# Weight preparation in shorter units over more rounds: a vision transformer on one core

## The chip, the core and the metric

The kernel runs on one core of one Trainium2 chip. The metric is the device time of one execution in microseconds (us). TensorE (PE) multiplies matrices into PSUM banks, VectorE (DVE), ScalarE (ACT) and GpSimd (POOL) work elementwise, SyncE (SP) issues the transfers; each engine runs its own instructions in order and waits on semaphores for the others.

## What is computed

64 images of 3x224x224 go through a small vision transformer: patches to 197 tokens of width 192, a first block (an attention with 64 queries and 133 keys, then an MLP whose weights are masked by mixed coefficients), and a second block (12-head attention, then a quantised MLP). Cut to what matters here:

```python
h = L0_tok(x)                                     # 64 x 197 x 192
h = h + L0_attn(layernorm(h))
h = h + L0_ffn(layernorm(h))                      # W0 = w_fc * C0, W1 = w_proj * C1
h = h + L1_attn(layernorm(h))                     # W_qkv, W_0
h = h + L1_ffn(layernorm(h))                      # clip(round(w / alpha)) for both weights
# C0 = sum over i, j of alpha_e[i] * alpha_r[j] * (row < r * e) * (col < e), C1 likewise
```

The weights are inputs, so their masks, sums, quantisation and splits are computed in the kernel as well. A value of 32 bits enters a product as a high part in 16 bits and a low part (value minus high part).

## The kernel before

`h` stays in SBUF for all images. Four stages follow one another: `embed_attend` (the fused stage: patch embedding and first attention), `mlp_0` (first MLP), `attention_1` and `mlp_1`. The first two handle two images in a round, 32 rounds each, and every engine has an order of jobs that it repeats each round, written out by hand (`PE_ORDER`, `ACT_ORDER`, `DVE_ORDER`, `POOL_ORDER`). A mark behind a job's name shifts it: `'` means that it handles the pair of one round later, `^` the pair of one round earlier. `rounds` writes these rounds out: those at the start and the end one by one, those between as a loop of two rounds a turn. Work that is not part of the rounds, the weight preparation, is hung behind a job as a unit: `{"a1": {6: mask_fp}}` runs `mask_fp` behind the job a1 of pair 6. The written-out part reaches to the last unit; the loop begins behind it.

In the fused stage ACT's h0 and h1 round the patches of image 0 and 1 to 16 bits (L357), POOL's l00 to l12 form their low parts in three operations an image (L314), PE's E0 and E1 multiply them (L442), VectorE's a0 and a1 add the position and write `h` (L596), b0 and b1 take statistics (L603) and r aggregates them (L612). Once in two rounds, for the odd pair, POOL waits behind l11 for r (L325, a_var) and computes the reciprocal root in fifteen small steps q1 to q15, with l12 behind q5; q15 ends with a_my. The attention jobs follow some rounds later: VectorE's m (maximum, L621, which waits for PE's scores s, L465), x, p, o, t, i, f, s. VectorE's order is `b1^ r^ i s f m x a0 p b0 o t a1`, so a unit behind a1 stands ahead of b1 and r.

The raw weights of that stage lie in the part of `h` that the rounds have not written yet, from image `RAW_FROM` on. SP loads two images a round and, behind given rounds, the raw masks and the quantisation inputs. ACT makes the high parts of the masked weights (`high_fc`, `high_fp`), VectorE the low parts (`low_fc`, `low_fp`).

In `mlp_0` VectorE's order is `n' w0 .. w5 x' f^`: x (L891, L892) takes the turned input from PSUM, the unit comes behind it, then f adds the result to `h` (L902), n normalises the next pair (L115, L117) and w forms low parts of the hidden values (L896). Units prepare the quantised weights of `mlp_1` (`scales` to `split_bias`; the last one releases SP's load of the raw qkv weights), then the low parts of the qkv weights (L874) and of the output weights (L867), whose high parts come from ACT's `high_qkv` and `high_wo` (L931), hung behind ACT's job u.

## Time and profile before

| | |
|---|---|
| median of 3 runs (lowest, highest) | 2665.69 us (2665.47, 2665.91) |
| the profiled execution, its span | 2663.56 us, 2661.8 us |
| PE busy | 2483.4 us (93%) |
| weight loads of PE (beside it) | 2115.2 us (79%) |
| DVE busy | 2208.2 us (83%) |
| ACT busy | 2087.4 us (78%) |
| POOL busy | 1088.0 us (41%) |
| mean granted TensorE clock | 0.975 |
| fused stage, first MLP | about 0 to 399 us, 399 to 800 us |

The profile is one execution. The span runs from its first instruction to its last; the execution's own time holds some 1.8 us around it. The granted clock is 1.00 at 2.4 GHz and 0.5 at 1.2 GHz; between them it is a mean over a stretch. Busy shares are means over four stages with different limits, so they don't say what a change in one of them is worth. "Idle before <- X" tells how long an engine had nothing to do before an instruction and what ended it.

### The profile page before, as it was taken

How to read it: one execution, taken by the hardware profiler on the slowest of the kernel's cores; microseconds unless marked ns; L12 is line 12 of the kernel's file. 1: busy time of each engine (PE TensorE's matmuls, PEld its weight loads, DVE VectorE, ACT ScalarE, POOL GpSimd, SP SyncE). 2: the span in 40 equal slices, each digit the busy share in tenths (PEclk: the TensorE clock that was granted, in tenths of full speed). 3: DMA queues.
4: the chain of work that ended last, by engine and by line, in shares of the span. 5: the costliest groups of instructions: out<-in, count | busy, mean ns of one | idle time of the engine just before them, and what ended most of it. 6: DMA issues, size and time to landing. Idle time of an engine off the chain costs nothing. (4 is left out here: it accounts for less than half of the span.)

```text
span 2661.8 us, 83340 instructions
## 1 busy us (share of the span) xinstructions
PE 2483.4 (93%) x27552; PEld 2115.2 (79%) x27552; DVE 2208.2 (83%) x5761; ACT 2087.4 (78%) x6199; POOL 1088.0 (41%) x1501
## 2 busy tenths in 40 slices
PE   5899968999997999999999999999999999997877
PEld 4788856877876888888888888888888888885665
DVE  6767668988766888888888888888888888886997
ACT  3777757777756888888888888888888888886998
POOL 6777723333322334333433433433333433441333
PEclk9999978999998999999999999999999999997999
DMA  5334400010002333333333333333333333330111
GB/s 176 104 109 117 120 23 9 0 45 0 0 0 64 76 78 72 68 82 68 68 82 68 69 81 69 72 77 73 72 73 77 72 70 80 70 69 10 44 42 50
DMA packets 181839, 173.22 MB, mean 65 GB/s; under 512 B 19206, under 2 KB 180432, under 8 KB 181520
## 3 DMA queue, kind: packets, MB, share of 16 engines
q1 hardware_dynamic: 181776, 172.44, 27.3%
q8 instruction: 32, 0.52, 0.1%
q14 instruction: 31, 0.25, 0.0%
HBM read 46.49 MB, written 9.68 MB: 21 GB/s over the span
## 5 line engine op out<-in xcount | busy, mean ns | idle before, releaser
L1347 POOL TENSOR_TENSOR b_pr<-b_pr,b_rinv 128x394 f32<-128x394 f32 (+1 forms) x768 | 626.2, 843 | 1006.6 <-DVE b_rinv L1305 1006.6
L1242 ACT ACTIVATE b_pr<-b_banks,b_nmx 128x197 f32<-128x197 f32 (+1 forms) x1536 | 625.9, 424 | 27.8 <-DVE b_nmx L1299 25.3
L1213 ACT ACTIVATE b_pt<-b_bank_t 128x394 f16<-128x394 f32 (+1 forms) x768 | 338.0, 494 | 202.6 <-PE b_bank_t L1178 202.4
L1299 DVE TENSOR_REDUCE b_nmx<-b_banks 128x2 f32<-128x394 f32 (+1 forms) x768 | 397.3, 558 | 65.2 <-PE b_banks L1168 57.1
L1270 DVE TENSOR_TENSOR b_pt<-b_bank_t,b_pt 128x394 f16<-128x394 f32 (+1 forms) x768 | 395.9, 556 | 18.2 <-ACT b_pt L1213 18.1
L1152 PE MATMUL b_banks<-b_xt,wqkv 128*128 128x197 f16 x3840 | 373.9, 249 | 4.4 <-DVE b_xt L1270 2.2
L1178 PE MATMUL b_bank_t<-ident,b_pr 128*128 128x128 f32 (+3 forms) x3072 | 341.9, 253 | 3.1 <-DVE b_pt L1270 3.0
L1152 PEld LDWEIGHTS b_banks<-b_xt,wqkv 128*128 128x128 f16 x3840 | 320.9, 98 | 25.6 <-issue 18.8
L1168 PE MATMUL b_banks<-b_kst,b_qst 128*128 128x197 f16 (+1 forms) x3072 | 326.8, 248 | 6.7 <-ACT b_pr L1242 4.6
L1178 PEld LDWEIGHTS b_bank_t<-ident,b_pr 128*128 128x128 f32 (+3 forms) x3072 | 282.1, 142 | 43.1 <-issue 35.3
L1242 ACT ACTIVATION_READ_ACCUMULATOR b_pr<-b_banks,b_nmx 128x1 f32 (+1 forms) x1536 | 315.6, 205 | 0.0
L1168 PEld LDWEIGHTS b_banks<-b_kst,b_qst 128*128 128x128 f16 (+1 forms) x3072 | 266.0, 105 | 19.4 <-issue 14.1
L1192 PE MATMUL b_bank_o<-b_pt,b_val 128*64 128x197 f16 (+1 forms) x4608 | 272.4, 253 | 0.1
L442 PE MATMUL tokens<-tok_w,parts 128*128 128x192 f16 (+1 forms) x2304 | 210.6, 253 | 56.4 <-POOL parts L314 56.4
L442 PEld LDWEIGHTS tokens<-tok_w,parts 128*128 128x128 f16 (+1 forms) x2304 | 196.8, 109 | 66.7 <-POOL parts L314 47.4
L923 POOL TENSOR_TENSOR h<-h,fp_bias 69x192 f32 (+3 forms) x128 | 133.4, 1071 | 278.0 <-DVE m_xn L117 278.0
L1289 DVE SCALAR_TENSOR_TENSOR b_qk<-b_banks,b_qk 128x394 f16<-128x394 f32 x384 | 209.6, 560 | 45.1 <-ACT b_qk L1227 31.6
L1192 PEld LDWEIGHTS b_bank_o<-b_pt,b_val 128*64 128x64 f16 (+1 forms) x4608 | 187.0, 110 | 75.0 <-issue 29.7
L1159 PE MATMUL b_banks<-wqkv,b_xt 128*128 128x384 f16 (+1 forms) x1280 | 242.5, 328 | 0.7 <-DVE b_qk L1289 0.4
L1227 ACT ACTIVATE b_qk<-b_banks 128x394 f16<-128x394 f32 x384 | 189.2, 507 | 33.2 <-PE b_banks L1152 28.4
L314 POOL TENSOR_TENSOR parts<-patches,parts 128x394 f16<-128x394 f32 x192 | 185.8, 998 | 49.4 <-ACT parts L357 49.4
L1202 PE MATMUL b_banks<-wo,b_ot 128*128 128x192 f16 (+1 forms) x2304 | 203.2, 248 | 1.3 <-DVE b_ot L1270 1.3
(227 smaller groups left out, 4429.3 us busy)
## 6 DMA issues: line engine op xcount, KB each, us to landing
b_qst<-b_qk SPq DMA_DIRECT2D x512, 147.8 KB, 2.6
b_kst<-b_qk SPq DMA_DIRECT2D x512, 73.9 KB, 2.3
patches<-in_x SPq DMA_DIRECT2D x64, 588.0 KB, 4.2
out<-z_res SPq DMA_DIRECT2D x32, 192.0 KB
out<-z_res SPq DMA_DIRECT2D x32, 103.5 KB
m_raw_weights<-in_wqkv SPq DMA_DIRECT2D x2, 1152.0 KB, 6.4
m_raw_weights<-in_w SPq DMA_DIRECT2D x2, 576.0 KB, 5.3
h<-in_fc SPq DMA_DIRECT2D x1, 768.0 KB, 5.8
```

The costliest lines, as they stand in the source:

```text
L442: last = t.matmul(tokens[m][0:ROWS[c], c * D:(c + 1) * D], parts[m][:, pa, k, COLS[c]], tok_w[:, pb, k, :], start=(k == 0 and n == 0), sto ...
L1152: last = t.matmul(out[:, g * SEQ:(g + 1) * SEQ], w[:, (2 * n + g) * P:(2 * n + g + 1) * P], x, start=(j == 0), stop=(j == 4))
L1159: last = t.matmul(out[0:ROWS[c], 0:VH], x[:, COLS[c]], w[:, col:col + VH], start=(j == 0), stop=(j == 4))
L1168: last = t.matmul(banks[0:ROWS[c], c, e * SEQ:(e + 1) * SEQ], qst[:, part, e, n, COLS[c]], kst[:, e, n, :], start=(part == 0), stop=(part ...
L1178: last = t.transpose(bank_t[0:ROWS[kc], kc, e * SEQ + c * P:e * SEQ + c * P + ROWS[c]], pr[n % 3][0:ROWS[c], c, e, COLS[kc]], S["ident"][0 ...
L1192: last = t.matmul(bank_o[e * DH:(e + 1) * DH, b, lo:lo + SEQ], val[odd][0:ROWS[kc], pa, kc, head * DH:(head + 1) * DH], pt[n % 2][0:ROWS[k ...
L1213: return nc.scalar.activation(dst, src, ACT.Copy)
L1242: last = nc.scalar.activation(pr[n % 3][0:ROWS[c], c, e, :], banks[0:ROWS[c], c, e * SEQ:(e + 1) * SEQ], ACT.Exp, bias=nmx[n % 2][0:ROWS[c ...
L1270: return v.tensor_tensor(dst, src, high, ALU.subtract)
L1289: v.scalar_tensor_tensor(out=qk[:, 1, :, n], in0=banks[:, k, 0:2 * SEQ].rearrange("p (g t) -> p g t", g=2), scalar=QK_SCALE, in1=qk[:, 0, ...
L1299: v.reduce_max(nmx[n % 2][0:ROWS[c], c, :], banks[0:ROWS[c], c, 0:2 * SEQ].rearrange("p (e t) -> p e t", e=2), AX.X, negate=True).then_inc ...
L1347: last = nc.gpsimd.tensor_tensor(p, p, inv, ALU.mult)
```

## The change

It moves the units and divides some of them.

- Fused stage, VectorE: units behind a0 in rounds 2 to 4 and behind a1 in rounds 1 to 11 become one unit a round behind a1, rounds 6 to 19. ACT's `high_fc` and `high_fp` go from rounds 7 and 9 to 14 and 16; SP's mask loads from behind round 1 to behind round 3, the quantisation loads from 3 to 5. The raw weights begin at image 38 instead of 14 and take the room of 24 images instead of 50.
- First MLP, VectorE: `scales`, both divisions, both quantisations and `split_bias` are divided, with the same instructions in the same order but for the two limits, which now come ahead of both roundings; 18 units where there were 11, behind x of pairs 1 to 18 instead of 1 to 11. The low parts of the qkv weights go from pairs 14 to 17 to 22 to 25, that of the output weights from 19 to 28.
- First MLP, ACT: the scaling of the keys in two units, behind u of pairs 21 and 22 instead of one behind 14; `high_qkv` from 15 to 18 to 23 to 26; `high_wo` from 20 to 28.
- What follows from `rounds`: VectorE's loop in the fused stage begins at round 20 instead of 12, ACT's at 17 instead of 10; in the first MLP, where they began at round 19, fewer than two turns are left and neither engine has a loop any more.

```diff
-    h, RAW_FROM, RAW_SIZE = S["h"], 14, 50 * 2 * D
+    h, RAW_FROM, RAW_SIZE = S["h"], 38, 24 * 2 * D
...
-                rounds(sp, ["d"], count, load, {"d": {1: load_masks, 3: load_quantised}}, first=3)
+                rounds(sp, ["d"], count, load, {"d": {3: load_masks, 5: load_quantised}}, first=3)
...
-                rounds(act, ACT_ORDER, count, job, {"h1": {7: high_fc, 9: high_fp}}, first=2)
+                rounds(act, ACT_ORDER, count, job, {"h1": {14: high_fc, 16: high_fp}}, first=2)
...
-                first_slot = {2: coefficient(1), 3: coefficient_sum(0), 4: hidden_columns}
-                second_slot = {1: coefficient(0), 2: coefficient(2), 3: coefficient_sum(1), 4: mask_fc, 5: mask_fc_bias, 6: mask_fp, 7: mask_fp_bias,
-                               8: low_fc(0), 9: low_fc(1), 10: low_fp, 11: means}
+                first_slot = {}
+                second_slot = {6: coefficient(0), 7: coefficient(1), 8: coefficient(2), 9: coefficient_sum(0), 10: coefficient_sum(1), 11: hidden_columns,
+                               12: mask_fc, 13: mask_fc_bias, 14: mask_fp, 15: mask_fp_bias, 16: low_fc(0), 17: low_fc(1), 18: low_fp, 19: means}
...
-                def divide_first():
-                    for k in range(2):
-                        then(v.tensor_tensor(r_w1[:, k], r_w1[:, k], a_w1[:], ALU.mult))
...
+                def divide_first(k):
+                    return lambda: then(v.tensor_tensor(r_w1[:, k], r_w1[:, k], a_w1[:], ALU.mult))
+
+                def divide_second(half):
+                    def make():
+                        for k in range(3 * half, 3 * half + 3):
+                            then(v.tensor_tensor(r_w2[:, k], r_w2[:, k], a_w2[:], ALU.mult))
+                    return make
...
-                units = {1: scales, 2: invert_rows(0), 3: invert_rows(1), 4: invert_rows(2), 5: invert_rows(3), 6: divide_first, 7: divide_second,
-                         8: quantise(0), 9: quantise(1), 10: sum_second, 11: split_bias, 19: low_wo}
-                units.update({14 + n: low_qkv(n) for n in range(4)})
+                units = {1: scales, 2: invert_scale, 3: invert_rows(0), 4: invert_rows(1), 5: invert_rows(2), 6: invert_rows(3), 7: divide_first(0),
+                         8: divide_first(1), 9: divide_second(0), 10: divide_second(1), 11: limit(0), 12: limit(1), 13: quantise(0), 14: quantise(1),
+                         15: sum_second, 16: divide_bias, 17: split_bias, 18: pick_bias, 28: low_wo}
+                units.update({22 + n: low_qkv(n) for n in range(4)})
...
-                        act.wait_ge(keys_scaled, 1)
+                        act.wait_ge(keys_scaled, k + 1)
...
-                rounds(act, ACT_ORDER, count, job, {"u": {14: scale_keys, 20: high_wo, **{15 + n: high_qkv(n) for n in range(4)}}}, first=2)
+                rounds(act, ACT_ORDER, count, job, {"u": {21: scale_keys(0), 22: scale_keys(1), 28: high_wo, **{23 + n: high_qkv(n) for n in range(4)}}}, first=2)
```

## Rows read from the trace of the kernel before

**Rows 1.** Windows by pair: length, busy PE PEld DVE ACT POOL (count), PEclk, DMA, GB/s.
```profile
34.34:59.86 25.52, 15.26 (x172) 14.27 (x172) 19.18 (x47) 11.88 (x19) 19.09 (x34) 0.93 0.35 97
59.86:82.92 23.06, 19.11 (x214) 17.25 (x215) 16.93 (x71) 13.19 (x26) 17.64 (x34) 0.85 0.37 106
82.92:106.42 23.50, 20.00 (x261) 17.86 (x259) 19.12 (x68) 17.89 (x33) 16.93 (x33) 1.00 0.37 104
128.80:152.75 23.95, 21.66 (x260) 19.41 (x258) 17.60 (x68) 16.43 (x32) 16.83 (x33) 0.93 0.36 101
152.75:174.32 21.57, 18.39 (x222) 16.37 (x221) 14.70 (x61) 14.01 (x27) 15.55 (x33) 0.92 0.34 96
174.32:194.76 20.44, 19.04 (x249) 16.90 (x247) 14.26 (x61) 15.88 (x31) 15.70 (x33) 1.00 0.41 117
```

**Rows 2.** Timeline of VectorE in a clean odd round: start, length, instruction, idle before.
```profile
208.59 0.30 DVE L621 TENSOR_REDUCE mx<-bank_s 128x1 f32<-128x133 f32 x1 [3.03 <-PE bank_s L465]
...
214.68 0.38 DVE L612 BATCH_NORM_AGGREGATE mv<-st 128x2 f32<-128x6 f32 x4
```

**Rows 3.** Timeline of GpSimd: a_var of the first pair, and a clean pair's first steps.
```profile
34.34 0.20 POOL L325 TENSOR_TENSOR a_var<-mv,a_eps 128x8 f32<-128x8 f32 x1 [1.72 <-DVE mv L612]
...
215.20 0.20 POOL L325 TENSOR_TENSOR a_var<-mv,a_eps 128x8 f32<-128x8 f32 x1 [0.43 <-DVE mv L612]
...
222.68 5.23 POOL L314 TENSOR_TENSOR parts<-patches,parts 128x394 f16<-128x394 f32 x6
```

**Rows 4.** Timeline of TensorE: E0 behind the clean pair's root steps.
```profile
225.38 3.14 PE L442 MATMUL tokens<-tok_w,parts 128*128 128x192 f16 x36 [1.01 <-POOL parts L314]
```

**Rows 5.** The tile parts over the fused stage: count, duration ns min/median/max, forms.
```profile
L314 POOL TENSOR_TENSOR parts<-patches,parts x192: 902/912/2812, 11.9 to 349.6; 128x394 f16<-128x394 f32 x192
L357 ACT ACTIVATE parts<-patches x64: 1173/1191/1192, 10.5 to 344.3; 128x1182 f16<-128x1182 f32 x64
```

**Rows 6.** Windows over eight units, VectorE alone: length, busy DVE (count), PEclk, DMA, GB/s.
```profile
29.89:33.03 3.14, 3.03 (x5) 1.00 0.76 239
34.62:36.66 2.04, 1.93 (x5) 1.00 0.00 0
43.46:47.53 4.07, 3.96 (x5) 1.00 0.27 55
50.04:54.23 4.19, 4.11 (x4) 1.00 0.45 138
55.32:58.56 3.24, 3.17 (x4) 1.00 0.57 181
61.47:64.89 3.42, 3.31 (x19) 0.54 0.00 0
70.82:72.56 1.74, 1.74 (x4) 1.00 0.59 143
80.04:81.66 1.62, 1.51 (x4) 1.00 0.60 136
```

**Rows 7.** Windows of the first MLP, from x' to x', columns as in the first.
```profile
426.51:775.02 348.51, 342.26 (x3205) 279.00 (x3203) 289.79 (x733) 258.33 (x529) 124.76 (x116) 1.00 0.02 9
438.92:473.85 34.93, 34.93 (x333) 28.72 (x332) 31.25 (x76) 26.04 (x55) 12.96 (x13) 1.00 0.01 1
520.42:559.59 39.17, 36.82 (x332) 29.95 (x331) 33.74 (x88) 26.04 (x55) 12.96 (x13) 0.96 0.16 60
571.23:633.68 62.45, 59.10 (x553) 47.57 (x551) 50.85 (x127) 47.61 (x95) 21.61 (x21) 1.00 0.03 10
633.68:646.43 12.75, 12.19 (x117) 9.82 (x115) 10.42 (x26) 9.72 (x20) 4.31 (x5) 1.00 0.00 1
646.43:763.45 117.02, 117.02 (x1103) 95.28 (x1101) 91.19 (x241) 86.81 (x181) 43.21 (x41) 1.00 0.00 0
```

**Rows 8.** Waits of VectorE in the first MLP: total us, times, longest us.
```profile
DVE wqkv L874 <- ACT wqkv L931: 7.5, 4, 1.9
DVE wo L867 <- ACT wo L931: 1.9, 1, 1.9
```

28 lines of the change are left out of this document (14 added, 14 removed).

## The prediction

> **What bounds the kernel now.** I read the profile in this order: the busy table and the granted clock for the whole span, then the stretches (busy time by window), then the timeline of the two stages that the change touches, then the waits of VectorE there. TensorE is busy 93% of the span, but not evenly, and the change touches only the first 800 us. About what a measurement of this kernel can tell from no change is 0.2%, here 5.3 us. The sum is made against the profiled execution (2663.56 us, span 2661.8); the median of the runs is 2.1 us above it, and I carry a difference in span over to the median unchanged.
>
> *Fused stage.* One round handles two images, and the norm statistics are handed to GpSimd once in two rounds, so I count in pairs, from one start of a_var (L325) to the next. A pair without units takes 20.44 us; the ones before it, which carry units or their aftermath, take 21.57 to 25.52 (six of them, five shown) [rows 1]. The clean pair shows which chain closes. TensorE's scores end and release VectorE's maximum at 208.59, after 3.03 us of idling; from there VectorE works without a pause through m, x, a0, p, b0, o, t, a1, b1 to the aggregate of r at 214.68 to 215.06 [rows 2]. GpSimd starts a_var at 215.20, works through the root steps until 222.68 and on into six parts operations [rows 3]; TensorE's next E0 starts when the third of them is done, at 225.38, and waited 1.01 us for it [rows 4]. From m to there it is 16.8 us; E0's 3.1 [rows 4] and the scores behind it close the loop at 20.4. That loop is the stage, and it has no slack where a1's unit of an **odd** round stands. A unit behind a1 of an **even** round stands between mv of r and the next m, where VectorE idles 3.03 us [rows 2]; it costs nothing up to that size, unless it slows GpSimd's parts operations, which it runs beside. These take 0.91 us at the median and up to 2.81 [rows 5].
>
> *First MLP.* VectorE is not the bound: in three rounds with a reciprocal unit each TensorE is busy all 34.93 us, 11.64 a round; ten loop rounds without units take 117.02, 11.70 each [rows 7].
>
> **The change, part by part.** *Taken out of rounds 1 to 4 (fused).* The units are measured as stretches in the first stage: coefficients 3.14, 2.04 and 4.07 us, the sums 4.19 and 3.24, hidden_columns 3.42, mask_fc 1.74 and mask_fc_bias 1.62 [rows 6]. Gone from these rounds, a_var of the first pair comes 1.7 us earlier (its whole idle time) [rows 3]. The next pair falls from 25.52 to about 20.0: the pipeline is still filling and VectorE's long chain is not there, so the lower end is 10.2 from a_var to E0 [rows 3, 4], E0 and E1 at 3.1, ACT's copy at 1.2 and two parts operations at 0.91 [rows 5], 19.5 in all; the clean 20.44 is the upper end, the one after from 23.06 to 20.44 [rows 1]. Together -9.8 us, bounds -8.5 to -10.5.
>
> *Put into rounds 6 to 12, one unit a round.* Here the pipeline is full. Even slots: coefficient(0) in 6 overflows its 3.03 us by 0.1 and slows a parts operation a little, 0.3; coefficient(2) in 8, 4.07 - 3.03 = 1.0; coefficient_sum(1) in 10, up to 4.19 beside GpSimd, 1.1; mask_fc in 12 fits, 0.3. Odd slots pay in full: coefficient(1) in 7, 2.0; coefficient_sum(0) in 9, 4.19 beside a busy GpSimd, but here GpSimd has run out of work and waits for VectorE, so 3.1 (3.24 for the same work as coefficient_sum(1), partly undisturbed [rows 6]); hidden_columns in 11, 3.4; mask_fc_bias in 13, 1.6 [rows 6] (before, in round 5, it was part of the 23.06). Sum 12.8. The longer odd units also open a TensorE gap behind which the granted clock falls to its lower level for a while, which shows as 0.92 or 0.93 in the pair: the pair of 21.57 has no unit at all, only that, and is 1.1 us over the clean one [rows 1]. Whether each of the three longest new ones brings one is not sure; three at 0.9 are 2.7. Eight more rounds of VectorE run unrolled instead of looped: -0.4 by the 0.055 a round of the MLP. Together +15.1, bounds +11 (sums at their undisturbed length, no lower clock) to +19.
>
> *Rounds 13 to 19.* Behind mask_fc_bias, mask_fp, mask_fp_bias, low_fc twice, low_fp and means follow one another in slots of the same parity as before in 6 to 11. So the four pairs that follow (82.92 to 174.32) are repeated eight rounds later and displace four clean ones: 0, give or take 1.5. ACT's high_fc and high_fp now come two rounds ahead of what reads them, and no wait was seen before. On SP's queue the seven mask loads move behind the patch load of round 3, and the four others behind that of 5: the transfers keep the DMA engines 0.34 to 0.37 busy in these pairs [rows 1], no wait for patches was seen in them, so 0. Fused stage: **+5.3**, bounds +0.5 to +10.
>
> Weighed against a page: the parts operation of 2.81 us is 1.9 longer than the median [rows 5], and mask_fc, an operation of 1.74, is the one unit long enough [rows 6]. The Trainium skill, SBUF — State Buffer, section "Who interferes with whom", says that such a VectorE operation holds a port pair for its whole length and GpSimd's fully blocks; by that rule a unit of an even round costs its length again when it meets the first three parts operations, instead of the 0.3 above. The trace agrees with it for that one operation; for the shorter ones the stretch shows less.
>
> *First MLP.* From the 3rd x' to the last, 29 rounds, it takes 348.51 us [rows 7]. Working from 11.64 a round: 337.7. The first of them has 0.8 more from the stage's start. The three rounds with sum_second and split_bias take 39.17, 4.2 above three clean ones; TensorE gets 36.82 busy of it and the clock falls to 0.96 [rows 7]. Split into three units of under 2 us each, in three rounds, it should vanish as the reciprocals do; I keep 0.1. The five rounds with low_qkv take 62.45, 4.2 too many, with VectorE waiting 1.9 us each for ACT's high copies [rows 7, 8]. Both sides move by eight rounds together, so this stays. low_wo waits 1.9 for high_wo [rows 8] and its round takes 12.75 [rows 7], 1.1 too many; now it stands a round behind the copy, so this goes. What remains of the loop, 11 rounds at 0.055, goes as well, since neither VectorE nor ACT keeps a loop. 337.7 + 0.8 + 0.1 + 4.2 = 342.8: **-5.7**, bounds -4.3 (0.7 kept by the split units, half of the loop's gain) to -6.8. Splitting the key scaling, the limits and the first divisions falls into VectorE and ACT time that is free at that point: 0. SP waits for quantised_done, seven rounds later than before, and again two rounds ahead of the ACT reader; nothing else is queued there.
>
> A second page speaks here. The ten loop rounds show no pause at the turn, TensorE is busy all 117.02 us [rows 7]. The Trainium skill, Runtime: NRT & Kernel Launch, section "Instruction fetch mechanics", says that a taken branch can force a fetch before execution goes on. By it six turns of VectorE's loop would each give back more than the 0.1 that I count; this trace does not show it.
>
> Sum: 5.3 - 5.7 = -0.4 us. Predicted **2665.3 us**.
>
> **Rivals.** (a) *GpSimd blocked.* The even units lengthen the first three parts operations, which lie on the closed loop: mask_fc 1.9, coefficients and the sum 0.7 each (an estimate, since the stretches of parts with such units beside them grew by less than one operation), coefficient_sum(0) takes its disturbed 4.19 (1.1 more), and one more pair has the low clock (1.1); that is +6.2, so 2671.5. It decides from the point where the fused stage loses 11 us. For it: the 2.81 and the pair of 25.52. Against: behind an odd unit with a low clock VectorE's even slot comes later, beside the operations that are not on the loop. (b) *Units absorbed.* VectorE is busy 14.26 of 20.44 us in a clean pair [rows 1], and the 23.5 us of new units are 5.9 a pair, which would just fit. Then rounds 6 to 12 cost 7 instead of 15, and the time is 2657. For: the totals. Against: the idle time is ahead of m, not behind a1 of odd rounds, and the pairs from 82.92 on grew by what stood there. (c) *The split gains nothing*: the MLP's rounds 10 to 12 are late for TensorE's own reasons, so the MLP gives 2 instead of 5.7, and the time is 2669.
>
> **How the numbers follow.** Forecast with the two stages cancelling: 0.58. (a) 0.15, (b) 0.20, (c) 0.07. The forecast's own bounds are 2660.5 to 2670. The range takes in most of (a) and reaches into (b): 2659.5 to 2671.5. Faster by over 0.2% (below 2660.4): 0.21, from (b) and a little of the forecast's edge. Slower (above 2671.0): 0.14, most of (a). Within: 0.65.
>
> **What would show it.** In the changed kernel a_var should come near 32.6, 53 and 73 instead of 34.34, 59.86 and 82.92; then pairs of 22.8, 25, 26 and 24 us; after it the same four lengths as before and clean 20.44 only from about 262, some 5 us behind. If these pairs are 21 to 22, (b) holds; if a parts operation of 2 us or more stands among the first three of a round, (a). In the MLP no round above 12 between the 10th and the 19th, four rounds of 12.8 at the 22nd to 25th, low_wo without a wait. I am wrong if the later stages move by more than 2 us, for instance by where the clock falls at their seams.

## The result, and the profile after

| | before | after |
|---|---|---|
| median of 20 runs each (lowest, highest) | 2665.4 us (2663.3, 2667.0) | 2669.4 us (2665.6, 2674.1) |
| profiled execution, its span | 2663.56 us, 2661.8 us | 2669.1 us, 2667.3 us |
| PE, DVE, ACT, POOL busy | 2483.4, 2208.2, 2087.4, 1088.0 us | 2487.0, 2210.0, 2087.4, 1084.0 us |
| mean granted TensorE clock | 0.975 | 0.974 |
| first m_xn of the MLP (end of the fused stage) | 400.91 us | 410.78 us |
| 3rd x' to the last x' of the MLP | 348.51 us | 342.79 us |

The ratio is 1.0017 with an interval of 1.001 to 1.0024: 4.0 us slower, where I had forecast 0.4 us faster. The time lies in the range, between the forecast (2665.3) and rival (a) (2671.5). Busy times hardly moved (DVE 2208.2 to 2210.0), so the time went into how the work meets. The MLP came out as forecast. The fused stage lost 9.9 us instead of 5.3, and the stages behind the MLP added another 1.3 in this pair of profiles, which differ by 5.5 us where the medians differ by 4.0.

The same windows as in [rows 1], from a_var to a_var, for the changed kernel. Columns: length, busy PE PEld DVE ACT POOL (count), PEclk, DMA, GB/s.

```profile
34.45:53.32 18.87, 14.86 (x163) 14.18 (x162) 6.68 (x32) 9.26 (x15) 14.42 (x35) 0.91 0.65 195
53.32:73.54 20.22, 17.04 (x224) 14.94 (x223) 11.43 (x49) 15.07 (x29) 15.77 (x34) 1.00 0.44 123
73.54:96.71 23.17, 21.82 (x280) 19.37 (x279) 19.46 (x67) 17.90 (x34) 16.08 (x34) 1.00 0.45 128
96.71:124.17 27.46, 22.32 (x236) 19.58 (x236) 21.61 (x68) 16.10 (x30) 15.65 (x33) 0.81 0.31 88
124.17:149.88 25.71, 20.83 (x272) 18.18 (x269) 21.93 (x82) 16.22 (x31) 17.25 (x34) 1.00 0.33 94
149.88:172.36 22.48, 18.93 (x223) 16.96 (x222) 17.63 (x65) 14.75 (x28) 16.90 (x34) 0.92 0.38 106
172.36:197.30 24.94, 21.72 (x261) 19.43 (x259) 19.72 (x70) 18.09 (x34) 16.72 (x33) 0.93 0.33 98
197.30:219.44 22.14, 19.38 (x234) 17.23 (x232) 16.64 (x63) 15.46 (x31) 16.75 (x34) 0.92 0.39 106
219.44:243.28 23.84, 20.43 (x265) 18.18 (x262) 17.85 (x68) 16.91 (x33) 16.89 (x34) 1.00 0.37 105
243.28:265.96 22.68, 19.51 (x222) 17.39 (x221) 14.55 (x61) 14.02 (x27) 15.59 (x33) 0.85 0.33 93
265.96:286.40 20.44, 19.04 (x249) 16.89 (x247) 14.15 (x61) 15.87 (x31) 15.70 (x33) 1.00 0.42 115
73.54:265.96 192.42, 164.94 (x1974) 146.33 (x1972) 149.38 (x537) 129.45 (x243) 131.82 (x264) 0.93 0.36 102
```

The filling rounds do what I forecast: the third a_var stands at 73.54 (forecast 73). So does the clean pair behind, 20.44. Of the eight pairs between, I had 22.8, 25, 26, 24 and then the four of before. They sum to 192.4 where my working gives 188.3. The excess sits in three pairs: 27.46, 24.94 and 22.68. All three show a lower PEclk than the pairs that I had taken as their model.

Windows over two of the six stretches of low granted clock between 80 and 260 us, same columns (the others are 153.8, 184.5 and 201.6, each 3.40 long as the second here, and 245.9, 6.80 long):

```profile
99.20:106.00 6.80, 5.70 (x36) 5.55 (x37) 2.56 (x9) 0.66 (x2) 5.49 (x17) 0.50 0.31 89
119.70:123.10 3.40, 3.40 (x28) 2.46 (x26) 3.29 (x7) 2.19 (x4) 0.00 (x0) 0.50 0.11 35
```

Both stretches lie in the pair of 27.46. The granted clock is 0.50 in them, 1.2 instead of 2.4 GHz, and PE is busy for most of the time. Together the six are 27.3 us long.

VectorE in that pair (timeline: start, length, instruction, idle before). L636 is job t, L523 and L524 are coefficient(2), L621 is m, L617 is x, L529 and L531 are coefficient_sum(0), and L465 on TensorE makes the scores:

```profile
106.80 0.29 DVE L636 COPY pt<-bank_p 64x256 f16<-64x256 f16 x1 [5.00 <-PE bank_p L474]
107.97 2.98 DVE L523 TENSOR_SCALAR h<-h,alpha 128x384 f32<-128x384 f32 x3
110.98 0.62 DVE L524 TENSOR_SCALAR h<-h,alpha 128x768 f32<-128x768 f32 x1
112.01 0.54 PE L465 MATMUL bank_s<-xt 96*64 96x133 f16 x12
113.99 0.30 DVE L621 TENSOR_REDUCE mx<-bank_s 128x1 f32<-128x133 f32 x1
114.39 2.42 DVE L617 TENSOR_TENSOR xs<-xn,xs 128x384 f16<-128x384 f32 x2
120.16 0.61 DVE L529 TENSOR_SCALAR h<-h,below 128x768 f32<-128x768 f32 x1
120.81 2.07 DVE L531 SCALAR_TENSOR_TENSOR h<-h,below 128x768 f32<-128x768 f32 x2
```

Job t, ahead of coefficient(2) of round 8, waits 5.00 us for TensorE at its low clock. The unit's 3.63 us then end in no idle time: m at 113.99 follows without a gap, where a clean round has 3.03 [rows 2], and starts 1.4 us behind the end of the scores (112.55). x behind it takes 2.42 us, where it takes 1.01 in a clean round. TensorE now waits for VectorE, for `prs`, at 117.68 for 2.04 us, a wait that I had not priced, and the next low stretch begins at 119.7. The sum of round 9 is only 2.7 long (I had 3.1), so its size is not what was wrong.

The first MLP, as in [rows 7]: the whole, the two rounds around sum_second, the four with low_qkv, and the one with low_wo.

```profile
436.44:779.23 342.79, 339.45 (x3203) 278.06 (x3201) 290.60 (x734) 258.47 (x529) 124.77 (x116) 1.00 0.03 9
601.27:624.64 23.37, 23.37 (x224) 19.23 (x222) 21.70 (x56) 17.71 (x38) 8.65 (x8) 1.00 0.00 0
670.79:721.92 51.13, 47.79 (x447) 38.32 (x445) 41.75 (x101) 38.92 (x77) 17.27 (x16) 1.00 0.04 12
744.87:756.57 11.70, 11.70 (x114) 9.63 (x112) 10.42 (x25) 8.67 (x19) 4.33 (x4) 1.00 0.00 0
```

TensorE is busy in all of the 23.37 us, at full clock, where the three rounds of before had 36.82 of 39.17. The low_qkv rounds still take 12.8 each. That of low_wo takes 11.70, without its wait.

### The profile page after: what moved, and what is told of

It reads as the page before. It is cut to its first block and busy times, and to the rows that moved or that the text cites. A ratio compares the mean times of both kernels' runs of the same rounds, so it can differ in the third digit from the quotient of the medians.

```text
span 2667.3 us, 82653 instructions
## 1 busy us (share of the span) xinstructions
PE 2487.0 (93%) x27552; PEld 2119.7 (79%) x27552; DVE 2210.0 (83%) x5761; ACT 2087.4 (78%) x6199; POOL 1084.0 (41%) x1501
## 3 DMA queue, kind: packets, MB, share of 16 engines
q1 hardware_dynamic: 181776, 172.44, 27.3%
## 5 line engine op out<-in xcount | busy, mean ns | idle before, releaser
L442 PE MATMUL tokens<-tok_w,parts 128*128 128x192 f16 (+1 forms) x2304 | 216.1, 257 | 55.3 <-POOL parts L314 55.2
```

What stands on the lines that cost most here:

```text
L442: last = t.matmul(tokens[m][0:ROWS[c], c * D:(c + 1) * D], parts[m][:, pa, k, COLS[c]], tok_w[:, pb, k, :], start=(k == 0 and n == 0), sto ...
```

## The experiments

Unless another base is named, diffs are against the changed kernel, cut to their core. Each expectation states the theories that it sets against each other. m_xn is the start of the first normalisation of the MLP (before 400.91, after 410.78). Times are medians, but e7, e8 and e11 were executed once each and e4 four times; a ratio is to the kernel before. A stretch comes from one profiled execution.

### One half of the change at a time

`e1_fused_alone`: the fused stage as changed, the MLP as before.

```diff
-                units = {1: scales, 2: invert_scale, 3: invert_rows(0), 4: invert_rows(1), 5: invert_rows(2), 6: invert_rows(3), 7: divide_first(0),
...
+                units = {1: scales, 2: invert_rows(0), 3: invert_rows(1), 4: invert_rows(2), 5: invert_rows(3), 6: divide_first, 7: divide_second,
```

> The change in the fused stage alone; the first MLP is that of the kernel before. Theory A (the stages add up: the fused stage lost 9.9 us up to the first m_xn, the MLP gained 5.7): 4 to 6 us more than the changed kernel, about 2674, ratio to before 1.003 to 1.0045. Theory B (the two parts disturb each other or the later stages, so that the parts don't add): the sum of this run's and the next one's difference from the kernel before is off from the changed kernel's 4.0 us by more than 2 us.

Measured: 2674.3 us beside 2665.1, ratio 1.0043 (1.0031 to 1.0055), as expected; m_xn at 412.7. Its eight pairs take 192.4 us as in the changed kernel. Its third a_var stands at 75.58 instead of 73.54, though the code up to there is the same: that is all of its later m_xn.

`e2_mlp_alone`: the reverse.

```diff
-                second_slot = {6: coefficient(0), 7: coefficient(1), 8: coefficient(2), 9: coefficient_sum(0), 10: coefficient_sum(1), 11: hidden_columns,
...
+                second_slot = {1: coefficient(0), 2: coefficient(2), 3: coefficient_sum(1), 4: mask_fc, 5: mask_fc_bias, 6: mask_fp, 7: mask_fp_bias,
```

> The change in the first MLP alone; the fused stage is that of the kernel before. Theory A: 5.7 us less than the kernel before, about 2659.7, ratio 0.9979; x' to x' 363.7 instead of 369.4 us, no round above 12.1 but the four with low_qkv. Theory B (writing the rounds out costs in the later stages what the MLP gains): 2663 or more.

Measured: 2661.3 us, ratio 0.9989 (0.998 to 0.9997). Same window and columns as above, from the 3rd x' to the last:

```profile
428.05:770.88 342.83, 339.49 (x3203) 277.92 (x3201) 290.48 (x734) 257.73 (x528) 125.26 (x116) 1.00 0.03 9
```

The stage gives its 5.7 us (348.51 to 342.83); of the whole, 3.8 come out, with an interval that reaches 5.3. The two halves by themselves, +9.2 and -3.8, add to +5.4 where the whole change shows +4.0: they don't act on each other by more than the measurement leaves open. 2661.3 lies between the two theories (2659.7, and 2663 or more). The loss is all in the fused stage, and what follows looks only there.

### The other parity, and no units

`e3_units_one_round_earlier`: every unit of the fused stage a round earlier, ACT's two copies with them.

```diff
-                second_slot = {6: coefficient(0), 7: coefficient(1), 8: coefficient(2), 9: coefficient_sum(0), 10: coefficient_sum(1), 11: hidden_columns,
...
+                second_slot = {5: coefficient(0), 6: coefficient(1), 7: coefficient(2), 8: coefficient_sum(0), 9: coefficient_sum(1), 10: hidden_columns,
...
```

> The changed kernel with every unit of the fused stage one round earlier (5 to 18), so that units of odd slots stand in even ones and the reverse; ACT's two copies go with them. Theory A (a unit behind an odd a1 pays its whole length, one behind an even a1 only what exceeds the idle time ahead of m): odd slots now hold coefficient(0) 3.4, coefficient(2) 3.6, coefficient_sum(1) 3 to 4, mask_fc 1.7 to 2, mask_fp 3.0, low_fc 0.9, low_fp 1.6 = 17 instead of 15 us, the even ones 3.6 us at most each: within 3 us of the changed kernel, but pairs change as the units do: those with mask_fp behind an odd round grow, those with mask_fp_bias behind an even one shrink to 20.5 to 21.5. Theory B (the parity doesn't matter, each unit adds a fixed share of its length): the pairs are as long as in the changed kernel in the same order, moved by half a pair.

Measured: 2671.5 us, ratio 1.0028 (1.0018 to 1.0038), m_xn at 415.3, 4.5 behind the changed kernel. From the second a_var it takes 215.6 us over nine more pairs where the changed kernel takes 212.6, so the other parity is no way out: whichever units stand in the odd rounds, the pairs grow. None of them fell to the 20.5 to 21.5 expected around mask_fp_bias in an even round; the shortest is 22.3. Most of the rest it loses behind them, where nothing but the loop is left, which here begins at an odd round. A pair there:

```profile
248.58:269.35 20.77, 19.22 (x249) 16.92 (x247) 14.88 (x61) 14.70 (x29) 15.45 (x33) 1.00 0.39 111
```

`e4_no_units`: the units left out, their waits kept; the masked weights are not computed.

```diff
-                second_slot = {6: coefficient(0), 7: coefficient(1), 8: coefficient(2), 9: coefficient_sum(0), 10: coefficient_sum(1), 11: hidden_columns,
...
+                second_slot = {6: only_wait, 19: only_wait_more}
```

> The changed kernel with no unit of the fused stage computed (coefficients, masks, low parts and means are left out: the low parts are zero, the means 1, the weights unmasked, so the output isn't the reference's); waits for the loads stay at slots 6 and 19. Theory A: pairs of 20.44 from the second on, fill as in the changed kernel (a_var near 34.5, 53.3, 73.5), the granted clock never low between 45 and 350 us, m_xn at 383 to 385 us: 26 us less than the changed kernel, nearly all of which is 17 (pairs of rounds 6 to 13) and 12 (14 to 21). Theory B (part of the loss is the longer written-out code or the later loads): some pairs between rounds 6 and 20 stay above 20.6 us without any unit.

Measured: 2640.6 us, ratio 0.9913 (0.9899 to 0.9927); m_xn at 378.44. Two windows, pair by pair as above, then the stretch of the eight pairs:

```profile
93.19:113.23 20.04, 19.03 (x249) 16.89 (x247) 13.97 (x61) 15.75 (x31) 15.58 (x34) 1.00 0.42 121
254.11:274.55 20.44, 19.04 (x249) 16.90 (x247) 14.15 (x61) 15.88 (x31) 15.70 (x34) 1.00 0.41 117
73.15:233.68 160.53, 152.54 (x1974) 135.41 (x1972) 111.48 (x479) 128.75 (x243) 124.30 (x264) 1.00 0.43 122
```

This gives two facts. By these profiles the units cost the stage 22.5 us before (400.91 - 378.44; some 1.6 of it are four more pairs in the loop) and 32.3 after. The profiled execution of e4 is the fastest of its four (2635.4; the median is 2640.6), and by medians the whole kernels differ by 28.8 where the profiles differ by 33.7, so a few us of these costs belong to the single execution. The lengths of pairs are firmer: bare pairs in the loop take 20.41 to 20.45 us in all profiles in which it begins at an even round. And a pair that is written out takes 20.04, one in the loop 20.44, with the same instructions: the base of my sum was 0.4 a pair too high wherever the rounds are written out. That is also why m_xn comes ahead of the 383 to 385 expected.

### Even units and odd units apart

`e7_even_units_only`: the units of rounds 6, 8, ..., 18 (those of the odd rounds are left out, so the weights are incomplete).

```diff
-                second_slot = {6: coefficient(0), 7: coefficient(1), 8: coefficient(2), 9: coefficient_sum(0), 10: coefficient_sum(1), 11: hidden_columns,
...
+                second_slot = {6: coefficient(0), 8: coefficient(2), 10: coefficient_sum(1),
+                               12: mask_fc, 14: mask_fp, 16: low_fc(0), 18: low_fp, 19: only_wait_more}
```

> The changed kernel with the units of rounds 6, 8, 10, 12, 14, 16 and 18 alone; those of the odd rounds are left out (coefficient(1), coefficient_sum(0), hidden_columns, both bias masks, the second low part of fc, means), so the output isn't the reference's. Theory A (an even unit costs what exceeds 3.0 us of idling, and what it does to GpSimd): 3 to 5 us above the kernel without units, m_xn at 381 to 384. Theory B (even units cost their length too): 12 us or more above it, m_xn above 390.

Measured: 2649.5 us, m_xn at 392.48: 14.0 us above no units, where my rule of free even slots gives 3 to 5. The pairs are 20.94, 21.40, 22.72, 23.22, 21.41, 20.72, 23.10 and 20.43. The pair with mask_fc, GpSimd behind its last root step (timeline: the answer of [rows 3] with its six operations), and mask_fc itself on VectorE:

```profile
138.90:162.12 23.22, 20.68 (x249) 18.47 (x247) 15.60 (x62) 15.78 (x29) 17.11 (x34) 0.93 0.38 101
...
146.27 6.75 POOL L314 TENSOR_TENSOR parts<-patches,parts 128x394 f16<-128x394 f32 x6
...
147.00 1.79 DVE L563 TENSOR_TENSOR h<-h 128x1536 f32<-128x1536 f32 x1
```

The six operations take 6.75 us instead of 5.23 [rows 3], and one of them 2.43, while mask_fc runs. Beside the other even units the same operations take 1.1 to 2.5; the first three of a round, for which E0 waits, take 6.8 us more over the eight pairs than in e4. So an even unit isn't free by itself: it hardly delays m (0.4 us in all), but it delays the parts operations that E0 waits for, and E0 is on the loop. The Trainium skill, SBUF — State Buffer, section "Who interferes with whom", says that a VectorE instruction with two SBUF inputs contends with a GpSimd instruction that reads SBUF, and that the one that comes second waits for the whole of the other. By that rule mask_fc costs up to its 1.79; the trace agrees, with 1.5 (2.43 - 0.91).

The parts operations are not the whole of the 14.0. Three of the pairs hold a stretch of low granted clock (22.72 at 0.92, 23.22 and 23.10 at 0.93), and E0 and the scores take 4.9 us more in them.

`e8_odd_units_only`: those of rounds 7, 9, ..., 19.

```diff
+                second_slot = {6: only_wait, 7: coefficient(1), 9: coefficient_sum(0), 11: hidden_columns,
+                               12: pass_on(1), 13: mask_fc_bias, 14: pass_on(2), 15: mask_fp_bias, 17: low_fc(1), 19: means}
```

> The changed kernel with the units of rounds 7, 9 to 19 alone; those of the even rounds are left out (coefficient(0) and (2), coefficient_sum(1), mask_fc, mask_fp, the first low part of fc, low_fp), so the output isn't the reference's. Theory A: their 15 us and the clock behind them, together 18 to 24 us above the kernel without units, m_xn at 396 to 402. Theory B (the loss needs both kinds together, since an even unit lies where the low clock has taken the idle time): this and the run with even units alone lose together 5 us or more less than the 32 us of the changed kernel.

Measured: 2659.0 us, m_xn at 401.6: 23.2 above no units, in the 18 to 24 expected. Its eight pairs and the second of them:

```profile
73.26:256.85 183.59, 161.21 (x1974) 143.66 (x1972) 130.06 (x522) 129.19 (x243) 125.16 (x264) 0.94 0.38 107
95.98:120.10 24.12, 20.71 (x258) 18.31 (x256) 17.64 (x64) 16.50 (x31) 15.68 (x34) 0.93 0.36 101
```

Odd units pay in full, as in my sum: the eight pairs are 23.1 us longer than in e4, for 18.6 us more of VectorE's work (130.06 against 111.48) and the low clock behind it.

The loop of a pair can be cut in five pieces, at starts and ends that the timelines give: the root steps (from a_var to the first parts operation of the odd round), the first three parts operations, TensorE (from there to the end of the scores, E0 in between), the wait until m starts, and VectorE (from m to the next a_var). In e4 the eight pairs of 160.5 us are 58.6, 21.1, 29.4, 0.3 and 51.2. What the others have more, in us:

| eight pairs | root steps | first three parts | TensorE | until m | VectorE | sum |
|---|---|---|---|---|---|---|
| even units alone (e7) | -0.1 | 6.8 | 4.9 | 0.4 | 1.4 | 13.4 |
| odd units alone (e8) | -0.3 | 0.0 | 7.2 | 0.0 | 16.2 | 23.1 |
| changed kernel | 0.1 | 2.3 | 9.0 | 2.8 | 17.7 | 31.9 |
| of it, rounds 6 to 12 | -0.4 | 0.4 | 3.7 | 2.8 | 12.1 | 18.6 |
| of it, rounds 13 to 19 | 0.4 | 1.8 | 5.3 | 0.0 | 5.6 | 13.3 |
| units behind f (e5, below) | 4.7 | 0.0 | 0.0 | 1.3 | 5.2 | 11.1 |
| even ones behind f (e11, below) | -0.2 | 0.0 | 0.0 | 1.4 | 4.7 | 5.9 |

The TensorE piece grows only where there is a stretch of low clock, so it is what the clock costs. And what even units do alone is not what they do in the changed kernel. There an even unit comes later, behind an odd one and the low clock, and most of them run beside later parts operations, for which E0 does not wait. mask_fc in the changed kernel (L563, VectorE), and the fifth parts operation of its round:

```profile
160.04 2.10 DVE L563 TENSOR_TENSOR h<-h 128x1536 f32<-128x1536 f32 x1
160.50 2.42 POOL L314 TENSOR_TENSOR parts<-patches,parts 128x394 f16<-128x394 f32 x1
```

The operation is as long as in e7, and it costs nothing here: the pair takes 22.48 us, as in e8, where mask_fc is left out. The price is paid elsewhere: m starts late behind coefficient(2) and coefficient_sum(1) (1.4 us each), and the x behind a late m meets the parts operations and is the one that waits: in the four odd rounds up to the 13th the two instructions of x take 7.6 us instead of 4.1. Apart, the two kinds add to 36.5 us in the pairs, together they cost 31.9: 4.5 less for the parts operations and 3.1 less for the clock, 2.4 more for m.

### The clock

`e6_tensor_kept_busy`: TensorE gets 8 to 28 multiplications of 192 columns behind s in seven odd rounds, into a bank that is written anew afterwards.

```diff
+                def keep_busy(n, p):
...
+                            t.matmul(tokens[1][:, 0:D], S["ident16"][:], tok_w[:, 0, 0, :], start=True, stop=True)
...
-                rounds(pe, PE_ORDER, count, job, first=2)
+                rounds(pe, PE_ORDER, count, job, {"s": {4: keep_busy(24, 8), 6: keep_busy(28, 10), 8: keep_busy(28, 12), 10: keep_busy(12, 14), 12: keep_busy(24, 16),
...
```

> The changed kernel with 8 to 28 extra matmuls of 192 columns on TensorE (into tokens[1], overwritten by E1) behind the scores of rounds 7, 9 to 19, that is in the gap in which it waits for GpSimd behind an odd unit. Theory A (the clock is the term that I undersized: 27 us in six low stretches): the low stretches between 90 and 250 us vanish, the eight pairs from round 6 on lose 5 to 9 us together, m_xn at 402 to 406. Theory B (the clock costs next to nothing since the chain runs over GpSimd and VectorE): the low stretches vanish and the pairs stay within 2 us of what they were, or grow by the extra matmuls.

Measured: 2666.0 us, ratio 1.0005 (0.9996 to 1.0014). The stretch of the eight pairs, the second and the last:

```profile
75.66:265.74 190.08, 173.56 (x2120) 153.90 (x2118) 148.59 (x537) 129.37 (x243) 131.32 (x265) 0.96 0.37 104
98.80:123.98 25.18, 21.73 (x248) 18.86 (x247) 22.07 (x68) 16.09 (x30) 16.26 (x33) 0.89 0.34 97
245.47:265.74 20.27, 18.73 (x244) 16.54 (x243) 14.55 (x61) 14.02 (x27) 15.53 (x34) 1.00 0.37 102
```

Two of the three pairs in excess are gone: 27.46 is 25.18, which is what my sum gave this pair, and 22.68 is 20.27. But over the eight pairs 2.3 us came back instead of the 5 to 9 expected, because low stretches appear elsewhere (145.7, 162.8 and 186.7). Filling some gaps moves the clock's fall as well as avoiding it. In this trace each stretch among the eight pairs follows an idle time of TensorE of 1.8 to 2.1 us, but one of 2.18 at 230.8 has none behind it, nor have those of 2.33 and 1.88 in e5 below: the length of one gap doesn't decide.

`e10_tensor_busy_in_more_gaps`: fillers also behind E1 in two rounds and ahead of E0 in three.

```diff
+                def turn(n, p):
...
+                            t.transpose(bank_p[:, 0, 0:P], S["ident16"][:], S["ident16"][:])
...
+                                                  "E1": {9: turn(28, 5), 11: turn(28, 7)},
+                                                  "m": {9: before_e0(14, 14), 11: before_e0(14, 16), 15: before_e0(18, 20)}}, first=2)
```

(against the kernel of e6)

> The run with extra matmuls, with more of them in the gaps that were left between 110 and 235 us (28 transposes behind E1 of rounds 9 and 11, 14 to 18 matmuls ahead of E0 in rounds 13, 15 and 19). Theory A (low stretches follow the gaps of 1.8 us and more, and each costs about 1.2 us; those left in the first such run came behind the gaps left open): at most one low stretch between 80 and 260 us, the eight pairs from round 6 on take 184 to 188 us together instead of 192.5 in the changed kernel and 190.0 in the first such run, kernel at 2661 to 2665. Theory B (what the pairs lose is the wait itself): 189 us or more together.

Measured: 2663.3 us, ratio 0.9986 (0.9976 to 0.9996).

```profile
73.44:260.60 187.16, 173.71 (x2222) 155.59 (x2220) 149.92 (x537) 129.40 (x243) 132.56 (x265) 0.99 0.38 105
```

One low stretch of 3.4 us is left between 80 and 260, of 27.3. The eight pairs take 187.2 instead of 192.4, in the 184 to 188 expected. So 24 us less at the low clock come with pairs 5.3 us shorter. By the five pieces TensorE gives 7.6 us back (9.0 to 1.4), while the first three parts operations take 2.1 more, most of it since mask_fc, no longer behind a low clock, meets the second of them. The three pairs in excess (27.46, 24.94, 22.68) are 25.18, 23.03 and 20.48; the pair with the stretch that is left, at 225.7, is the only one that grew much (23.84 to 25.21). By halves: the first four pairs take 96.4 instead of 98.8, the other four 90.7 instead of 93.6. The same units at the same places now make a kernel that is not slower than before.

### The loop

`e9_fused_written_out`: VectorE's and ACT's rounds of the fused stage all written out.

```diff
-                rounds(dve, DVE_ORDER, count, job, {"a0": first_slot, "a1": second_slot}, first=2)
+                rounds(dve, DVE_ORDER, count, job, {"a0": first_slot, "a1": second_slot}, first=32)
...
-                rounds(act, ACT_ORDER, count, job, {"h1": {14: high_fc, 16: high_fp}}, first=2)
+                rounds(act, ACT_ORDER, count, job, {"h1": {14: high_fc, 16: high_fp}}, first=32)
```

> The changed kernel with VectorE's and ACT's rounds 20 (17) to 31 of the fused stage written out too, units as they were. Theory A (a pair in the loop takes 20.44 us, a written-out one 20.05, as in the kernel without units; a loop turn costs 0.4): the last pairs fall to 20.05, the stage's end comes 2.0 to 3.0 us earlier, the kernel takes 2666 to 2668. Theory B (20.05 belongs to rounds of the first half only, whatever the code's form): no change above 0.5 us.

Measured: 2665.4 us, ratio 1.0003 (0.9994 to 1.0012). A pair of the part that was the loop:

```profile
266.00:286.04 20.04, 19.03 (x249) 16.89 (x247) 13.96 (x61) 15.76 (x31) 15.58 (x34) 1.00 0.44 120
```

It takes 20.04 instead of 20.44. Five or six such pairs should give some 2 us, and from the end of the eight pairs to m_xn it is 143.1 instead of 144.8; between the two medians lie 4.0, and the intervals of the two ratios meet, so the rest may be chance.

This run shows something else. Up to round 17 its code is that of the changed kernel, and yet the pair with mask_fp (24.94 there, with PEclk 0.93) is this one:

```profile
175.03:198.28 23.25, 20.06 (x261) 17.85 (x259) 19.68 (x70) 18.07 (x34) 16.68 (x33) 1.00 0.38 105
```

The first four pairs take 98.8 us in both, the last four 91.0 here and 93.6 there; 1.5 of the difference is the TensorE piece (18.5 and 20.0), and what the loop gives in the last of these pairs is some 0.4. So the clock can fall at other places in another execution of the same instructions, and a pair is then up to 1.7 us longer or shorter.

### The place in the round

`e5_units_behind_f`: the same units in the same sequence, hung behind f instead of a1. Each stands five jobs later, still ahead of the same m, but behind b1, r, i, s and f of the next round (f handles the pair of six rounds earlier, so `1` is round 7). The hand-over of the statistics, b1 and r, now comes first.

```diff
-                second_slot = {6: coefficient(0), 7: coefficient(1), 8: coefficient(2), 9: coefficient_sum(0), 10: coefficient_sum(1), 11: hidden_columns,
...
+                behind_f = {1: coefficient(0), 2: coefficient(1), 3: coefficient(2), 4: coefficient_sum(0), 5: coefficient_sum(1), 6: hidden_columns,
...
-                rounds(dve, DVE_ORDER, count, job, {"a0": first_slot, "a1": second_slot}, first=2)
+                rounds(dve, DVE_ORDER, count, job, {"f": behind_f}, first=2)
```

> The changed kernel with the same units in the same rounds, but hung behind VectorE's job f (directly ahead of m) instead of behind a1, that is three to five jobs later, past b1, r, i, s and f. Theory A (a unit behind an odd a1 holds up r and so GpSimd's root steps, and through them TensorE and its clock): odd units cost only what exceeds the 1.6 us that VectorE idles there, pairs of rounds 6 to 20 fall from 22 to 27.5 us to 20.1 to 22, low stretches of the clock all but vanish there, the first m_xn comes at 385 to 392 us instead of 410.8 and the kernel takes 2645 to 2653. Theory B (VectorE's total time is what counts: 34 us of units in 32 rounds, wherever they stand): less than 4 us better than the changed kernel.

Measured: 2650.0 us, ratio 0.9945 (0.9931 to 0.9958), 19.4 below the changed kernel. The first three of the eight pairs (compare 23.17, 27.46, 25.71), and one of the loop, which begins at an odd round here:

```profile
73.49:94.32 20.83, 19.60 (x253) 17.30 (x251) 17.02 (x63) 16.55 (x32) 15.59 (x33) 1.00 0.49 138
94.32:116.06 21.74, 19.22 (x249) 16.92 (x247) 20.82 (x69) 16.34 (x31) 16.75 (x34) 1.00 0.38 108
116.06:140.03 23.97, 19.27 (x248) 16.90 (x247) 22.37 (x67) 16.82 (x33) 18.77 (x33) 1.00 0.38 108
...
265.89:286.67 20.78, 19.22 (x250) 16.92 (x247) 14.94 (x61) 15.87 (x31) 15.45 (x34) 1.00 0.40 115
```

VectorE does 20.82 us of work in a pair of 21.74. An even unit still lies in the idle time ahead of the same m, but beside later parts operations; behind an odd one r has already been handed over, so the root steps run meanwhile. The granted clock does not fall between 41 and 352 us. m_xn is at 391.1, in the 385 to 392 expected. So most of the loss came from the place: the eight pairs cost 11.1 us more than bare ones where they cost 31.9. These 11.1 are still paid for the amount. Units beside the root steps lengthen them (4.7 us; single steps of 0.20 take up to 0.91), and x takes 12.9 us instead of 8.1 in the odd rounds.

`e11_even_units_behind_f`: e7's even units alone, behind f, VectorE's rounds written out to round 27 (the odd units are left out).

```diff
-                second_slot = {6: coefficient(0), 8: coefficient(2), 10: coefficient_sum(1),
...
+                behind_f = {1: coefficient(0), 3: coefficient(2), 5: coefficient_sum(1),
+                            7: mask_fc, 9: mask_fp, 11: low_fc(0), 13: low_fp, 14: only_wait_more}
```

(against the kernel of e7)

> The seven even units alone, as in the run with even units only, but behind f instead of behind a1, so that they start when GpSimd has the first parts operations of the round behind it; VectorE's loop begins at round 28 or later. Theory A (14 us for even units come from the parts operations l01 and l02 that they lengthen, on the closed loop, and from the length beyond 3 us): these two keep 0.91 us, mask_fc, mask_fp and the low parts cost nothing, m_xn at 380 to 384 instead of 392.5. Theory B (the even units cost VectorE time as such): m_xn at 388 or more.

Measured: 2639.1 us, m_xn at 382.82 instead of 392.48; some 2 us of that is the loop. Seven of the eight pairs take 20.07 to 21.03, one 21.95. The same units lengthen parts operations here too, but those late in a round, l11 and l12, and not l01 and l02, for which E0 waits. Less the loop, some 7.7 of the 14.0 us that the even units cost behind a1 hang on that place, and they are both the parts operations (6.8 to 0.0) and the clock (4.9 to 0.0), less what x pays more here.

### Two attempts at a better placement

`e12_units_in_idle_time`: the two first coefficients behind b0 of round 2, the others behind f from round 3 on, mask loads two rounds earlier, ACT's copies behind h1 of rounds 8 and 10, VectorE and ACT written out.

```diff
+                behind_b0 = {2: both(coefficient(0), coefficient(1))}
+                behind_f = {-3: coefficient(2), -2: coefficient_sum(0), -1: coefficient_sum(1), 0: hidden_columns, 1: both(mask_fc, mask_fc_bias),
+                            3: mask_fp, 4: low_fc(0), 5: mask_fp_bias, 6: low_fc(1), 7: low_fp, 9: means}
...
-                rounds(sp, ["d"], count, load, {"d": {3: load_masks, 5: load_quantised}}, first=3)
+                rounds(sp, ["d"], count, load, {"d": {1: load_masks, 3: load_quantised}}, first=3)
```

> A version put together from what the runs showed: the two first coefficients behind b0 of round 2, where VectorE idles 5.7 us while the pipeline fills, the others behind f of rounds 3 to 15 by their size against the idle time there (3.0 and 1.6 us in full rounds, 2.2 to 4.6 in filling ones), mask loads behind round 1 again, VectorE and ACT written out in the fused stage, the MLP as in the changed kernel. Theory A: first m_xn at 378 to 384 us, kernel 2637 to 2643, 22 to 28 us less than before. Theory B (filling rounds are no cheaper than full ones): no better than 2648.

Measured: 2647.5 us, ratio 0.9933 (0.992 to 0.9946): the best complete kernel of the study, 18.0 below before, yet short of the 2637 to 2643 expected. m_xn stands at 390.35, not 378 to 384. The pair with the coefficients, one with units, and a clean one:

```profile
33.14:56.23 23.09, 15.62 (x167) 14.94 (x166) 17.98 (x46) 9.69 (x15) 17.47 (x34) 0.85 0.40 109
...
101.44:121.45 20.01, 18.65 (x245) 16.51 (x243) 17.03 (x64) 15.94 (x31) 16.29 (x33) 1.00 0.36 99
187.12:207.12 20.00, 18.63 (x244) 16.49 (x243) 13.95 (x61) 14.94 (x30) 15.55 (x33) 1.00 0.40 107
```

A full pair with mask_fp, 3.1 us of VectorE's time, takes 20.01, as long as one without a unit: behind f a unit can be free. But the miss is larger than that gain. In the filling rounds the first pair takes 23.09 and the clock falls; the idle time that the totals show there is not idle at the place of the units, which cost about 8 us in these rounds. And two later pairs take 22.03 and 22.84, with units of 0.9 to 3.1 us in them and a low stretch in the second.

`e13_matched_to_idle_time`: units cut smaller and put behind f in rounds 6 to 23, each about as long as the idle time ahead of m; ACT's copies behind h1 of rounds 17 and 20; written out.

```diff
+                in_round = {6: coefficient(0, 0), 7: both(coefficient(0, 1), coefficient(1, 0)), 8: coefficient(1, 1), 9: coefficient(2, 0),
...
+                            18: low_fc(0), 19: mask_fp, 20: low_fc(1), 21: mask_fp_bias, 22: low_fp, 23: means}
```

> The units of the fused stage behind f in rounds 6 to 23 (none in the filling rounds), coefficients, sums and hidden_columns cut so that odd rounds get up to 3.0 us and even ones up to 1.7, VectorE and ACT written out there, the MLP as in the changed kernel. Theory A (only what exceeds the idle time ahead of m costs, and a written-out pair takes 20.05): pairs of 20.05 to 21.0 throughout, no low stretch of the clock between 80 and 340 us, first m_xn at 378 to 382, kernel 2636 to 2641. Theory B (34 us of units cost at least a third of their length wherever they stand, as in the runs with units behind f so far): m_xn at 387 or later, kernel 2646 or more.

Measured: 2654.4 us, ratio 0.9954 (0.994 to 0.9967), m_xn at 396.18, not 2636 to 2641.

```profile
97.36:118.98 21.62, 19.22 (x249) 16.92 (x247) 17.88 (x65) 15.83 (x31) 16.63 (x33) 1.00 0.39 110
140.71:162.53 21.82, 19.29 (x249) 16.92 (x247) 18.65 (x64) 15.83 (x31) 17.53 (x34) 1.00 0.39 110
```

Neither pair has a low clock, both have units that should fit, and both are 1.6 to 1.8 us over 20.04. Shorter units over more rounds pay this in more pairs. The five pieces say where: in the first of the two pairs the root steps take 8.16 us instead of 7.38, and VectorE from m to a_var 7.05 instead of 6.32. Both come from VectorE and GpSimd meeting (L523 is the unit, L333 and L335 are root steps, 0.20 us each when undisturbed; L620 is x):

```profile
98.35 0.51 DVE L523 TENSOR_SCALAR h<-h,alpha 128x576 f32<-128x576 f32 x1
98.38 0.53 POOL L333 TENSOR_SCALAR a_y<-a_var 128x8 int32<-128x8 int32 x1
99.07 0.50 POOL L335 TENSOR_TENSOR a_t<-a_y 128x8 f32<-128x8 f32 x1 [0.15 <-POOL a_y L333]
112.34 1.73 DVE L620 TENSOR_TENSOR xs<-xn,xs 128x384 f16<-128x384 f32 x2
112.72 2.12 POOL L314 TENSOR_TENSOR parts<-patches,parts 128x394 f16<-128x394 f32 x2 [1.64 <-ACT parts L357]
```

A parts operation starts at 112.72, just ahead of the second instruction of x, which then takes 1.26 us instead of 0.55. In e12's pair of 20.01 the two start within 0.02 us of each other (115.98 and 116.00) and the parts operation waits instead, which costs nothing there; x takes 1.01, the root steps 7.34.

## Why the prediction was wrong

The total moved by +4.0 where I had -0.4. By stage, in the profiles: fused +9.9 (I had +5.3), MLP -5.7 (-5.7), behind them +1.3 (0), 5.5 in all. So one term failed by 4.6 us, and it can be laid out along the stage:

| stretch of the fused stage | forecast | measured | off by |
|---|---|---|---|
| filling, to the third a_var | 73.1 us | 73.54 us | +0.4 |
| rounds 6 to 12, four pairs | 96.9 | 98.8 | +2.0 |
| rounds 13 to 19, four pairs | 91.4 | 93.6 | +2.2 |
| the rest, 265.96 to m_xn | 144.8 | 144.8 | 0.0 |

*Filling, -9.8.* Right in sum (-9.4), with some luck. The first a_var did not come earlier, 34.45 instead of 32.6, but the pair behind it was 18.87 instead of 20.4. In other runs with the same filling rounds the third a_var stands at 75.6 to 76.2 (e1, e6, e9, e13), a gain of only 6.7 to 7.3, outside my bounds.

*Odd units pay in full.* Right: alone they are 10.6 us of VectorE's piece in rounds 6 to 12, where my sum has 10.1. The sum of round 9 was sized 0.4 too large.

*Even units are free up to 3.03 us.* Wrong, the step that failed first. I gave them 2.7 us in rounds 6 to 12, 2.2 of it for what exceeds the idle time ahead of m; that is 2.8. What I had at next to nothing is how VectorE and GpSimd hold each other up: x behind a late m waits for the parts operations (VectorE's piece is 1.5 us longer than with odd units alone), and the first three parts operations grow by 0.4. That makes 4.7, 2.0 too little. In rounds 13 to 19 low_fp meets the second parts operation (2.02 us instead of 0.91), which it did not do before: 1.1 more. By themselves the even units cost 14.0 (e7). Rival (a), to which I gave 0.15, names the right pair of engines, and e7 shows its mechanism, but it is not what the changed kernel pays: there the first three parts operations lose 2.3 us in eight pairs, where rival (a) has 4.0 for the even units in the first four alone. What I had held against it came true: behind a low clock the even unit comes later, beside operations that are not on the loop, as mask_fc does (2.42 us for the fifth operation). The one operation of 2 us among the first three is low_fp's (2.02).

*Three low-clock stretches at 0.9, 2.7.* Sized too small: TensorE's piece grows by 3.7 in these four pairs, 2.4 of it in the pair of 27.46 alone, which has 10.2 us of low clock. The late m of that pair is not the clock's doing: it is 1.4 us behind the scores there, and as much in e10 without the low clock.

*Rounds 13 to 19 repeat four pairs of before, 0 give or take 1.5.* Outside its bounds, +2.2. The same units stand in the same parity, but the clock's falls are not carried along. Before has 10.2 us of low clock between 80 and 260, my sum implied three stretches more, 20.4; after has 27.3. The pair with mask_fp has a stretch now (0.93 against 1.00 [rows 1]) and is 1.4 longer; the last pair has 6.8 us of it (0.85 against 0.92) and is 1.1 longer. TensorE's piece makes 1.7 of the 2.2 (20.0 against 18.3 in the same pairs of before). This part differs between executions: e1 has the same 93.6, but e9, whose code is the same up to round 17, has 91.0 and a TensorE piece of 18.5.

*Written-out rounds, -0.4 by the 0.055 of the MLP.* Wrong in size, and for the better: a pair written out takes 0.40 less than one in the loop (e4, e9), 1.6 for the four new ones, 1.2 more than I took off. I took the price from the wrong stage. In the MLP TensorE hides the turn, here VectorE and GpSimd are the bound. The page of the Trainium skill that I had weighed, Runtime: NRT & Kernel Launch, "Instruction fetch mechanics", says that a taken branch can stop execution until its target is fetched. The trace agrees in direction, with 0.40 us for a turn of two rounds; that these 0.40 are a fetch no run shows. In the MLP the trace did not speak for more than the 0.1 that I had. So the first four pairs close: +2.0 for even units, +0.5 for odd ones, +1.0 for the clock, -1.2 for the loop and -0.4 for shorter root steps are +1.9, the 2.0 of the table.

*MLP, -5.7.* Right, and by its own steps: the split rounds at 11.64, the four low_qkv rounds still at 12.8, low_wo without a wait. Rival (c) gives nearly the measured total (2669) and is refuted all the same: a total can't choose between causes.

*Rival (b), units absorbed.* It was given 0.20 and is wrong for this placement (pairs of 22 to 27, not 21 to 22), but e5 shows that its price was sound for another place: the same units behind f cost 7.2 us in the first four pairs, where rival (b) has 7.

## What to carry to other kernels

Side work in an engine that follows a fixed order is priced by its place more than by its length: the same units differ by 19 us between two places of VectorE's order, five jobs apart. To price a place, ask both when the next job of this engine becomes late and whose instructions run beside it. Ask this with all the units in place: each of them moves the next, and a unit that alone met an operation of the closed loop met another one here. A loop cut in pieces at its hand-overs shows which piece a unit lengthens, where busy times and the sum of a pair do not. And a pair length read from one trace holds the clock's falls of that trace; subtract them before you move it elsewhere.
